# Two wide attention stages: values stationary instead of probabilities, and the output projection scaled after it

## What is computed

```
layer 0: xn = layernorm(layernorm(x)) * gamma;  q, k, v = xn @ w_q, xn @ w_kv (16 heads of 64)
         q, k normalised to length 1, scaled; two extra "null" keys and values per head
         sim = 8 q k^T + slope_h * (-|i - j|), causal;  out = softmax(sim) v;  x += out @ w_out
layer 2: q, k, v = x @ W_qkv + b_qkv;  attention = softmax(q k^T / 8) (not causal)
         x += (attention v) @ W_out + b_out
```

## Time and profile before

| | before |
|---|---|
| median of the runs | 2880.18 us |
| the profiled execution | 2880.27 us |
| its span, first to last instruction | 2878.6 us |
| mean granted TensorE clock | 0.944 |
| TensorE busy | 2569.0 us (89%) |
| VectorE busy | 1655.5 us (58%) |
| ScalarE busy | 1441.0 us (50%) |
| GpSimd busy | 1072.0 us (37%) |
| ps<-V,P matmuls | 3584 records, 434.7 us |

### The profile page before, as it was taken

How to read it: one execution, slowest core, us unless ns; L and a number is a source line. 1 busy time by engine, 2 the same in 40 slices (tenths; PEclk the granted TensorE clock), 3 DMA queues, 4 the chain that set the end, 5 groups by cost and what they waited for, 6 DMA issues and landing times. The chain is left out here.

```text
span 2878.6 us, 59759 instructions
## 1 busy us (share of the span) xinstructions
PE 2569.0 (89%) x23527; PEld 2158.5 (75%) x23527; DVE 1655.5 (58%) x4590; ACT 1441.0 (50%) x3049; POOL 1072.0 (37%) x1762
## 2 busy tenths in 40 slices
PE   4999999999987788889998999999999668888855
PEld 3999999999975455567777999999999665555533
DVE  4666666666647577645444666666665214555548
ACT  3555555555544567644444545545544223555631
POOL 4554555555526444334330111111111125455454
PEclk8999999999999699999999999999999886899976
DMA  3790000000000100000000000000000440000000
GB/s 104 242 320 2 2 2 2 2 2 2 2 1 1 48 2 2 2 1 21 1 1 3 3 5 5 3 5 5 3 5 5 147 131 14 6 7 5 1 1 29
DMA packets 22953, 82.47 MB, mean 29 GB/s; under 512 B 4082, under 2 KB 10868, under 8 KB 21652
## 3 DMA queue, kind: packets, MB, share of 16 engines
q1 hardware_dynamic: 19524, 71.44, 7.6%
q0 software_dynamic: 3152, 7.21, 0.8%
HBM read 71.44 MB, written 46.79 MB: 41 GB/s over the span
## 5 line engine op out<-in xcount | busy, mean ns | idle before, releaser
L2350 PE MATMUL ps<-V,P 128*128 128x65 f32 x3584 | 434.7, 273 | 0.0
L2350 PEld LDWEIGHTS ps<-V,P 128*128 128x128 f32 x3584 | 421.0, 192 | 0.1
L559 ACT ACTIVATE P<-ps 128x384 f32<-128x384 f32 (+1 forms) x512 | 250.9, 542 | 236.3 <-PE ps L2350 236.3
L1227 DVE TENSOR_REDUCE qa<-ps 128x2 fp32r<-128x512 f32 x256 | 176.4, 689 | 217.0 <-PE ps L2350 213.8
L1150 ACT ACTIVATE P<-ps 128x768 f32<-128x768 f32 x256 | 207.7, 812 | 148.2 <-PE ps L2350 145.9
L2350 PE MATMUL ps<-mk,identb 128*128 128x256 bf16 (+1 forms) x1024 | 202.4, 301 | 62.3 <-DVE qa L1228 61.3
L676 DVE TENSOR_REDUCE sm<-ps 128x2 f32<-128x512 f32 (+1 forms) x256 | 130.7, 552 | 177.3 <-PE ps L2350 177.3
L2366 POOL TENSOR_SCALAR stat<-stat 128x1 f32<-128x1 f32 x256 | 61.8, 242 | 421.5 <-DVE stat L2361 420.2
L1318 POOL TENSOR_SCALAR_AFFINE_SELECT P<-P 128x512 f32<-128x512 f32 x256 | 163.3, 638 | 137.1 <-ACT P L1150 136.5
L659 DVE TENSOR_REDUCE nm<-ps 128x2 fp32r<-128x512 f32 x256 | 164.4, 685 | 54.8 <-PE ps L2350 52.7
L780 POOL TENSOR_TENSOR ss<-ss,nhalf 128x16 f32<-128x16 f32 x64 | 187.9, 2935 | 5.3
(11 more groups left out here) (303 smaller groups left out, 7280.2 us busy)
## 6 DMA issues: line engine op xcount, KB each, us to landing
rows_i<-in_zero SPq DMA_DIRECT2D x16, 1208.0 KB, 30.9
rows_o<-in_zero SPq DMA_DIRECT2D x16, 1208.0 KB, 80.1
w<-in_m_w SPq DMA_DIRECT2D x23, 578.0 KB, 4.1
zt<-rows_i SPq DMA_DIRECT2D x23, 128.0 KB, 3.1
rows_o<-yo POOLq DMA_DIRECT2D x23, 128.0 KB, 3.9
stg<-in_t_w SPq DMA_DIRECT2D x11, 256.0 KB, 2.7
XR<-in_x SPq DMA_DIRECT2D x4, 512.0 KB, 8.6
out<-XR SPq DMA_DIRECT2D x8, 256.0 KB, 2.0
```

Of the source, the lines that this page charges most:

```text
L559: e.activation(self.P[at % 6][:, :], K.ps.ap("st", s, g, h)[:, 0:self.w], ACT.Exp, bias=0.0, scale=1.0 if kind == 0 else 0.125).then_inc(K ...
L1227: e.tensor_reduce(nm[:, 1], ps[:, :, 0:256], X, ALU.max, negate=True)
L2350: return self.te.matmul(o, l, r, start=start, stop=True, skip_group_check=True)
```

## The change

In both wide stages V becomes the stationary operand and P the moving one, 256 queries at a time. A head has 64 channels, so two heads are put side by side in the array's column halves and write partitions 0 to 63 and 64 to 127 of one bank. The result has channels on the partitions, as the projection needs it, and isn't transposed any more; ScalarE copies it to OT. The sums are products of their own: 32 columns of ones are stationary and four heads stand side by side. ScalarE copies the sums to S, TensorE transposes them (two, part "sT"), and VectorE takes the reciprocals, which now have queries on the partitions. As the result isn't divided before the projection, the projection is done for each head by itself: `pe_out` has two heads in the array's row halves, each with a bank Y. VectorE scales both banks, out of PSUM into T, and GpSimd adds the four slices of T to XR, unit by unit. Bank y goes, and the ring has eight banks. The bias of kind 2 is made once (`pe_bias`) and added to XR by GpSimd when a sequence has been normalised (`pool_bias`). The table of ticks changes with it: in kind 2 "pv" is one part at tick 11 (it was two at 10 and 11), in kind 0 one at 20 (two at 19 and 20), and a unit lives 14 and 23 ticks (16 and 24). The next stage starts a sequence when GpSimd has summed it.

```diff
         if kind == 0:
-            first, last, unit = 8, 9, 24
-            self.tk = {"qk": 0, "turn": 6, "mx": 9, "v": 12, "mT": 15, "st": 17, "pv": 19, "OT": 22, "out": 23}
+            first, last, unit = 8, 9, 23
+            self.tk = {"qk": 0, "turn": 6, "mx": 9, "v": 12, "mT": 15, "st": 17, "pv": 20, "sT": 21, "out": 22}
         else:
-            first, last, unit = 6, 5, 16
-            self.tk = {"turn": 0, "v": 2, "mx": 4, "mT": 6, "st": 8, "pv": 10, "OT": 13, "out": 15}
+            first, last, unit = 6, 5, 14
+            self.tk = {"turn": 0, "v": 2, "mx": 4, "mT": 6, "st": 8, "pv": 11, "sT": 12, "out": 13}
...
-        self.V = [sb(f"V{s}_{i}", [128, 2, 4, 65], F32) for i in range(4)]
-        self.O = [sb(f"O{s}_{i}", [128, 2, 256], F32) for i in range(3)]
-        self.rs = [sb(f"rs{s}_{i}", [128, 2, 2], F32) for i in range(2)]
-        self.hi_in, self.ones, self.op, self.z_hi, self.kb_in = (
-            K.sem(f"{n}{s}") for n in ("hi_in", "ones", "op", "z_hi", "kb_in"))
+        self.S = [sb(f"S{s}_{i}", [128, 256], F32) for i in range(2)]
+        self.T = [sb(f"T{s}_{i}", [128, 2, 2, 2, 128], F32) for i in range(2)]
+        self.rs = [sb(f"rs{s}_{i}", [128, 8], F32) for i in range(2)]
+        self.one = sb(f"one{s}", [128, 128], F32)
...
-    G, AC = (0, 1, 2, 3, 4, 5, 6), (7,)
-
+    G = (0, 1, 2, 3, 4, 5, 6, 7)
+
+    def done(self, b):
+
+        return self.summed, 4 * b + 4
...
-        n = self.part("pv", k)
-        if n is not None:
-            self.pe_pv(pe, g, u, n)
-        if self.part("OT", k) is not None:
-            ps = K.ps.take(pe, self.G, "OT", s, g)
-            O = self.O[g % 3]
-            for pr in range(2):
-                pe.wait_ge(*K.ps.read("pv", s, g, pr))
-                for i in range(2):
-                    p = K.tr(ps[:, 256 * pr + 128 * i:256 * pr + 128 * i + 128], O[:, i, 128 * pr:128 * pr + 128])
-            p.then_inc(K.ps.full_of("OT", s, g), 1)
+        if self.part("pv", k) is not None:
+            self.pe_pv(pe, g, u)
+        if self.part("sT", k) is not None:
+            ps = K.ps.take(pe, self.G, "sT", s, g)
+            pe.wait_ge(*K.ps.read("sm", s, g))
+            for i in range(2):
+                p = K.tr(ps[:, 128 * i:128 * i + 128], self.S[g % 2][:, 128 * i:128 * i + 128])
+            p.then_inc(K.ps.full_of("sT", s, g), 1)
         if self.part("out", k) is not None:
-            y = K.ps.take(pe, self.AC, *self.y(b)) if u == 0 else K.ps.ap(*self.y(b))
...
-            pe.wait_ge(*K.ps.read("OT", s, g))
-            if u == 0 and kind == 2:
-                pe.wait_ge(self.one_in, 1)
-                pe.wait_ge(*K.ps.read("beff"))
-                for i in range(2):
-                    K.acc(y[:, 128 * i:128 * i + 128], self.one[:, :], self.beff[:, :], start=i == 0)
-            for i in range(2):
-                for pr in range(2):
-                    p = K.acc(y[:, 128 * i:128 * i + 128], self.OT[g % 2][:, pr, 128 * i:128 * i + 128],
-                              K.wO[:, 256 * u + 128 * pr:256 * u + 128 * pr + 128],
-                              start=kind == 0 and u == 0 and i == 0 and pr == 0)
-            p.then_inc(self.op if u < 3 else K.ps.full_of(*self.y(b)), 1)
+            self.pe_out(pe, g, u)
...
-    def pe_pv(self, pe, g, u, pr):
+    def blocks(self):
+
+        return ((0, 0, 0, 256), (1, 128, 256, 128)) if self.causal else ((0, 0, 0, 256), (1, 0, 256, 256))
...
+    def pe_pv(self, pe, g, u):
         K, s, kind, V = self.K, self.s, self.kind, self.V[g % 4]
-        pv = K.ps.take(pe, self.G, "pv", s, g, pr)
+        pv, sm = (K.ps.take(pe, self.G, name, s, g) for name in ("pv", "sm"))
-            pe.wait_ge(self.nvs_in, 3)
-            for qt in range(2):
-                K.acc(pv[:, 130 * qt:130 * qt + 130], self.pnT[g % 2][:, 128 * qt:128 * qt + 128],
-                      self.nvs[:, 0, 260 * u + 130 * pr:260 * u + 130 * pr + 130], start=qt == 0)
+            for pr in range(2):
+                c = 256 * u + 128 * pr
+                K.acc(pv[:, 256 * pr:256 * pr + 256], self.nvs[:, 0, c:c + 128], self.pnT[g % 2][:, :], start=pr == 0)
+            K.acc(sm[:, 0:256], self.nvo[:, 4 * u:4 * u + 4, :].rearrange("p h c -> p (h c)"), self.pnT[g % 2][:, :],
+                  start=True)
...
-        pe.wait_ge(self.ones, 4)
-        for par in range(2):
-            h = 2 * pr + par
+        for h in range(4):
             pe.wait_ge(*K.ps.read("st", s, g, h))
-            PP = self.P[(4 * g + h) % 6]
-            for qt in range(2):
-                blocks = [(0, 128 * qt)]
-                if not self.causal:
-                    blocks.append((1, 256 + 128 * qt))
-                elif qt == 1:
-                    blocks.append((1, 256))
-                o = pv[:, 130 * qt + 65 * par:130 * qt + 65 * par + 65]
-                for n, (kt, c) in enumerate(blocks):
-                    p = K.acc(o, PP[:, c:c + 128], V[:, kt, h, :], start=kind == 2 and n == 0 and qt == 0 and par == 0)
-        p.then_inc(K.ps.full_of("pv", s, g, pr), 1)
+        P = [self.P[(4 * g + h) % 6] for h in range(4)]
+        for pr in range(2):
+            for kt, q, c, w in self.blocks():
+                for par in range(2):
+                    p = K.acc(pv[64 * par:64 * par + 64, 256 * pr + q:256 * pr + q + w], V[:, kt, 2 * pr + par, :],
+                              P[2 * pr + par][:, c:c + w], start=kind == 2 and kt == 0 and pr == 0)
+        p.then_inc(K.ps.full_of("pv", s, g), 1)
+        for kt, q, c, w in self.blocks():
+            for h in range(4):
+                p = K.acc(sm[32 * h:32 * h + 32, q:q + w], self.one[:, 0:32], P[h][:, c:c + w],
+                          start=kind == 2 and kt == 0)
+        p.then_inc(K.ps.full_of("sm", s, g), 1)
+
+    def pe_out(self, pe, g, u):
+
+
+        K, s, OT = self.K, self.s, self.OT[g % 2]
+        Y = [K.ps.take(pe, self.G, "Y", s, g, par) for par in range(2)]
+        pe.wait_ge(*K.ps.read("pv", s, g))
+        for pr in range(2):
+            for i in range(2):
+                for par in range(2):
+                    r = slice(64 * par, 64 * par + 64)
+                    p = K.acc(Y[par][:, 256 * pr + 128 * i:256 * pr + 128 * i + 128], OT[r, pr, 128 * i:128 * i + 128],
+                              K.wO[r, 256 * u + 128 * pr:256 * u + 128 * pr + 128], start=pr == 0 and i == 0)
+                    if pr == 1 and i == 1:
+                        p.then_inc(K.ps.full_of("Y", s, g, par), 1)
...
-                    ac.wait_ge(*K.ps.filled("pv", s, (at - 6) // 4, (at - 6) % 4 // 2))
+                    ac.wait_ge(*K.ps.filled("sm", s, (at - 6) // 4))
...
-        if self.part("OT", k) is not None:
+        if self.part("pv", k) is not None:
             if g >= 2:
-                ac.wait_ge(*self.out_done(g - 2))
-            ac.wait_ge(*K.ps.filled("OT", s, g))
-            e.activation(self.OT[g % 2][:, :, :].rearrange("p a c -> p (a c)"), K.ps.ap("OT", s, g)[:, :],
-                         ACT.Copy).then_inc(K.ps.out_of("OT", s, g), 1)
+                ac.wait_ge(*K.ps.filled("Y", s, g - 2, 1))
+                ac.wait_ge(*K.ps.filled("sT", s, g - 2))
+            ac.wait_ge(*K.ps.filled("pv", s, g))
+            e.activation(self.OT[g % 2][:, :, :].rearrange("p a c -> p (a c)"), K.ps.ap("pv", s, g)[:, :],
+                         ACT.Copy).then_inc(K.ps.out_of("pv", s, g), 1)
+            ac.wait_ge(*K.ps.filled("sm", s, g))
+            e.activation(self.S[g % 2][:, :], K.ps.ap("sm", s, g)[:, 0:256], ACT.Copy).then_inc(K.ps.out_of("sm", s, g), 1)
...
-        n = self.part("pv", k)
-        if n is not None:
-            self.dve_pv(dv, g, n)
-        if self.part("out", k) is not None and u == 3:
-            xs = K.XR[:, 2 * b:2 * b + 2, :].rearrange("p t c -> p (t c)")
-            dv.wait_ge(*K.ps.filled(*self.y(b)))
-            e.tensor_tensor(xs, K.ps.ap(*self.y(b))[:, 0:256], xs, ALU.add).then_inc(K.ps.out_of(*self.y(b)), 1)
+        if self.part("sT", k) is not None:
+            dv.wait_ge(*K.ps.filled("sT", s, g))
+            e.reciprocal(self.rs[g % 2][:, :], K.ps.ap("sT", s, g)[:, 0:256].rearrange("p (a c) -> p a c", c=32)[:, :, 0]
+                         ).then_inc(K.ps.out_of("sT", s, g), 1)
+        if self.part("out", k) is not None:
+            if g >= 2:
+                dv.wait_ge(self.summed, g - 1)
+            dv.wait_ge(*K.ps.read("sT", s, g))
+            r = self.rs[g % 2][:, :].rearrange("p (t a r) -> p r a t", t=2, a=2)
+            for par in range(2):
+                dv.wait_ge(*K.ps.filled("Y", s, g, par))
+                e.tensor_tensor(self.T[g % 2][:, par], K.ps.ap("Y", s, g, par)[:, :].rearrange("p (a t c) -> p a t c", a=2, t=2),
+                                r[:, par].unsqueeze(3).to_broadcast([128, 2, 2, 128]), ALU.mult).then_inc(
+                    K.ps.out_of("Y", s, g, par), 1)
...
-    def dve_pv(self, dv, g, pair):
-        K, s, e = self.K, self.s, dv.e
-        rs, O = self.rs[pair], self.O[g % 3]
```

(97 more changed lines are left out.)

12 lines of the change are left out of this document (6 added, 6 removed).

## The result

| | before | changed kernel |
|---|---|---|
| median of the runs | 2879.60 us | 2978.32 us |
| from ... to | 2872.95 to 2884.50 | 2972.95 to 2984.12 |
| ratio to before, 95% interval | | 1.0345 [1.0316, 1.0373] |
| span of the profiled execution | 2878.6 us | 2971.3 us |
| stage 0, first to last ident,nm | 773.4 us | 761.0 us |

What follows compares the result with a forecast made beforehand. TensorE's instructions were taken to bound both wide stages, as long as nothing they wait for comes late. From 2880 us: -19 (stage 0), +80 (stage 4), +4 (ends) = 2945 us; range 2870 to 3010.

Steps and rivals of the forecast that it cites:

- the likeliest case: Whole kernel: the forecast itself, 2905 to 2965 us, chance 0.50.
- rival 3: GpSimd late in stage 0, or TensorE's clock falling in stage 4: together 2965 to 3010 us, chance 0.2.
- TensorE's instructions, -0.85 a unit: Stage 4: TensorE's own instructions sum to 9.46 us a unit, 0.85 less than before.
- First and second wait: Stage 4, each unit: TensorE waits 1.52 us before transposing the maxima, 0.64 us before transposing the sums.
- the unit of 11.62: Stage 4: unit cycle of 9.46 + 1.52 + 0.64 = 11.62 us, against 10.31 before.
- Against the bias matmuls that go I call it even: Stage 4, every fourth unit: normalisations lengthen the first wait by 1.36 us, taken as even with the dropped bias matmuls.
- Clock at 1.00 in stage 4: Stage 4: the sum included no fall of TensorE's clock; 27 us over 16 sequences stood only in rival 3.
- Stage 0, -19: Stage 0: TensorE's instructions 0.3 us less a unit, no new waits, 64 units: -19 us.
- Ends, +4: Ends of the two wide stages: 5.8 us and not 3.9 to the next stage's first statistics, twice +1.9: +4 us.
- Rival 1: Both wide stages: TensorE's instruction sum decides and the two stage 4 waits are hidden: 2811 us, chance 0.13.

Runs made afterwards that it cites:

- e6: Changed kernel with GpSimd's residual adds in stage 0 cut to one channel of 128: 2977.37 us, 1.0332 of the kernel before.
- e11: e1 with P,V in both stages waiting for its exponentials two heads at a time, not all four: 2817.05 us, 0.9789 of the kernel before.
- e1: Changed kernel with stage 4's attention times values at tick 10 and not 11: 2822.93 us, 0.9831 of the kernel before.
- e12: Changed kernel with GpSimd's residual adds in stage 4 cut to one channel of 128: 2951.01 us, 1.0296 of the kernel before.
- e10: Changed kernel with 26 unused bf16 identity products in one stage 4 unit of four, in the rank unit's wait: 2966.14 us, 1.0298 of the kernel before.
- e4: Changed kernel with the dispatch of a sequence one tick later: 2965.65 us, 1.0336 of the kernel before.
- e7: Changed kernel with stage 4 left as in the kernel before, so the change is in stage 0 alone: 2866.35 us, 0.9945 of the kernel before.

## Why the prediction was right in sign and 33 us low

The measured 2978 lies inside the range of 2870 to 3010 but not in the likeliest case's own 2905 to 2965: it is where rival 3 stood, 2965 to 3010, which had a chance of 0.2. Of rival 3's two causes the fall of TensorE's clock in stage 4 came, and GpSimd was not late in stage 0 (e6). The path of the forecast, the two waits and what releases them, was right; these are its terms.

- **TensorE's instructions, -0.85 a unit: -0.65.** P,V and the projection cost what they were given. With all waits covered (e11) a plain unit is 9.66 against 9.46. Half of the difference is tick C, 1888.88 - 1887.83 = 1.05 where the forecast had 0.94: 0.09 of it is the switch to column halves behind the value projection (1888.67 to 1888.88 and not 0.12), which was not priced.
- **First and second wait, 1.52 and 0.64: 1.31 and 0.60.** Both are where the walk put them, and e1 shows the cause, since one tick takes both away. The first is 0.2 shorter, as the two scalings follow each other at 0.60 and not at the 0.68 of one record, and start earlier too. That and the dearer instructions cancel: the unit of 11.62 came out at 11.56 with each part a little off, which is luck.
- **"Against the bias matmuls that go I call it even": failed, 8 us.** I priced the four normalisations ahead of the scaling at 1.36; they lengthen their unit by 0.4 (to 12.0). They take 1.03 in VectorE's queue (1895.38 to 1896.41), and 0.6 of it is time in which VectorE would have waited for ScalarE's QH anyway. I didn't ask what else stands in VectorE's queue there once a sequence. It is the rank chain, 2.1 in the 13.7 us unit, of which 0.9 is lent to GpSimd's adds (e12); what went was the 1.7 by which before's fourth unit was longer. So 0.4 + 2.1 - 1.7 = +0.8 a sequence, 11 in 14 of them, less 3 for plain units that grew by 1.25 and not 1.31: measured without clock falls (e10) stage 4 grows by 762.2 - 674.0 = 88, forecast 80.
- **Clock at 1.00 in stage 4: failed, 16 us.** It was in rival 3 (27 us over 16 sequences) and not in the sum. Seven units are 1.6 longer and two 2.6, which makes these 16. All nine stand behind the longest wait, so whoever misses the rank chain misses this too. The chain isn't the only way to it: in e4, without that wait, the clock falls as well.
- **Stage 0, -19: right in kind, -12 measured.** Its four distances are 12.0, 12.0, 12.4, 12.7 (12.2, 12.2, 12.4, 12.9 before): 0.2 a unit and not 0.3. TensorE doesn't wait, as said, and e7 gives the stage's gain by itself. TensorE's sum was 0.1 too small.
- **Ends, +4: some 8.** At the end of stage 0 it is 6.95 us from P,V's end to the first statistics, where the forecast had 5.8: its list starts at the copy of the sums and leaves out the 0.9 of the sums themselves. P,V also stands later in the last unit, so that from the last ident,nm on the end costs 4.2 more than before; stage 4's costs 3.7 more, a figure with the experts' stage in it and less sure.

Together 80 + 8 + 16 for stage 4, -12 for the other, 8 for the ends, 100 where the forecast had 65; the medians of the runs give 98.7. Rival 1's time, 2811, was that of the same instructions with their cover. The runs at that level are e1 and e11, 2823 and 2817.

## What to carry to other kernels

Where engines go through their queues in a fixed order of ticks, what a change saves in instructions is less than what it can lose by the cover that the moved instructions gave: list for each transpose or copy what stands between producer and consumer on either engine, before and after, for the plain unit and for each unit that carries extra work. When a wait appears on TensorE, first try to move the block by one tick. Of the unit that waits most, ask also what a fall of the clock behind it would cost.
